# Retention heads in pairs, one in each 64-row half of TensorE's array, with one row tile moved from ACT to DVE

## The chip, the cores and the metric

The kernel runs on one core of a Trainium2 chip. The metric is the device time of one execution in microseconds (us). Before the change three runs took 2376.03, 2383.02 and 2388.97 us; the median is 2383.02. TensorE (PE) multiplies matrices into PSUM, VectorE (DVE) and ScalarE (ACT) read PSUM, GpSimd (POOL) works on SBUF, and SyncE (SP) issues most DMAs.

## The reference, cut to what matters

The program is a stack of eight layers on a sequence of 2048 tokens with 128 channels: softmax attention, a spline network, retention, the spline network again, linear attention, attention with a mixture of experts, a scan over time, and attention with experts again. The change touches the retention layer alone. For each of its 16 heads it needs, with q and k of 8 channels a head and a causal decay,

```
scores[t, s] = q[t] . k[s] * decay[t - s] / scale[t]        for s <= t, else 0
den[t]       = clip(sum over s of |scores[t, s]|, 1, 50000)
out[t]       = (sum over s of scores[t, s] * v[s]) / den[t]
```

followed by a norm over each head's 16 values and a gate. The decay is folded into q and k beforehand. The products with v of earlier token tiles come from a running state in an earlier stage; the stage changed here computes the sums of absolute values (they have no such short form, so every score below the diagonal is made) and the products with v of each token's own 128-token tile.

## The kernel before, in words

`retention_heads_stage` (L1727) takes the heads one after the other. The sequence is cut into 16 row tiles of 128 tokens. q and k of a head are split into high and low parts and so fill 32 rows (`KROWS`) of SBUF; rows 32 to 127 of `qm` and `km` are zero, and each product runs over all 128 rows of the array. There are two buffers, one a head, chosen by `par`.

For one head PE makes three kinds of products:

- "a" units (L1873): one row tile against up to 1024 earlier tokens, into one of two PSUM slots of two banks. ACT sums their absolute values in place (L1920). There are 11: row tiles 5 to 15.
- "d" units, into a ring of three PSUM banks (`DRING`). The first four hold the 16 diagonal tiles, four in a bank (L1883); DVE masks them into `sm` (L1949). The other 14 are what ACT doesn't take, up to 512 columns each (L1887): row tiles 1 to 4, and the part beyond 1024 tokens of row tiles 9 to 15. DVE sums their absolute values (L1955).
- the head's own output (`own_out`, L1852 and L1853): products of the masked scores and of their positive parts with v. They are made a head late, in four pieces, one behind each of d units 8 to 11 of the next head, in 32-column strips of the array. ACT copies the result (L1912), PE turns it with four transposes (`turn_out`, L1861, behind d unit 14), and DVE adds it to `ret` (`take_out`, L1940 and L1941, behind d unit 16).

PE's order is one written list, `order`: the a units are spread evenly among the d units. An a unit waits until ACT has read the unit two before it; a d unit waits until DVE has read the unit three before it. PE executes in this order, so a wait for one of them holds up everything behind it, the pieces of `own_out` too.

SP loads each head's rows with four DMAs (L1789, L1790) of 16 rows of 8 KB; before loading into a buffer it waits until PE is done with the head two before. The first two heads' loads are issued when the stage begins, and PE starts on a head when its four have landed (L1865). POOL makes the positive parts (L1827) and multiplies the gate (L1820).

The attention stages, which the change does not touch, keep two heads at a time in SBUF rows 0 to 63 and 64 to 127 and run products of 64 rows in either half of the array; lines L1175 and L1223 are theirs, and the trace shows their form as 64*128.

Of the kernel before, what the change touches and what calls it, by code (L numbers as in the profile page):

```python
# [18 lines left out]
ALU = mybir.AluOpType  # L19
# [80 lines left out]
def rounded(ap):  # L100

    return ap.bitcast(F32R)
# [1624 lines left out]
def retention_heads_stage(k, w, v, parts_dram, part, diag, ret, gate, x):  # L1727
# [21 lines left out]
    with ExitStack() as ctx:  # L1749
# [17 lines left out]
        PADDED = (slice(KROWS, 2 * KROWS), slice(2 * KROWS, P))  # L1767
# [11 lines left out]
        with nc.Block() as block:  # L1779

            @block.sync
            def _(sp):
                def body(h, par, first=False):
                    if not first:
                        sp.wait_ge(a_full.sem, a_full.at(h * NA - NA))
                        sp.wait_ge(d_full.sem, d_full.at(h * NV - NV))
                    for a in range(PARTS):
                        at = slice(a * PARTS * D, (a + 1) * PARTS * D)
                        sp.dma_start(qm[at, par, :], bcast(q_rows[h, a], 0, PARTS)).then_inc(loaded[par].sem, 16)  # L1789
                        sp.dma_start(km[at, par, :], k_rows[h]).then_inc(loaded[par].sem, 16)  # L1790

                wait_parts(sp, stored)
                body(0, 0, first=True)
                body(1, 1, first=True)
                with sp.Fori(1, H // 2) as n:
                    for par in range(2):
                        body(2 * n + par, par)

            @block.gpsimd
            def _(pool):  # L1800
                for par in range(2):
                    for n, rows in enumerate(PADDED):
                        nc.gpsimd.memset(km[rows, par, :], 0.0).then_inc(k_padded.sem, 1)
                        pool.wait_ge(k_padded.sem, k_padded.at(2 * par + n + 1))
                nc.gpsimd.memset(part[:], 0.0).then_inc(cleared.sem, 1)
                pool.wait_ge(cleared.sem, cleared.at(1))
                nc.gpsimd.memset(twice[:], 0.0).then_inc(cleared.sem, 1)
                pool.wait_ge(cleared.sem, cleared.at(2))
                nc.gpsimd.memset(twice[:, VD:VD + 1], 2.0).then_inc(cleared.sem, 1)
# [6 lines left out]
                def gate_head(h):  # L1816

                    pool.wait_ge(o_used.sem, o_used.at(2 * h + 1))
                    g, r = (t[:, :, bass.ds(h * VD, VD)] for t in (gate, ret))
                    nc.gpsimd.tensor_tensor(g, g, r, ALU.mult).then_inc(gated.sem, 1)  # L1820

                def body(h, par, first=False):
# [3 lines left out]
                    nc.gpsimd.tensor_copy(vh[:, par, :, 0:VD], v[:, :, bass.ds(h * VD, VD)]).then_inc(v_ready.sem, 1)  # L1826
# [3 lines left out]
                body(0, 0, first=True)  # L1830
                body(1, 1, first=True)
                nc.gpsimd.tensor_tensor(x[:], x[:], bcast(w["b_o"][:], 1, NT), ALU.add).then_inc(biased.sem, 1)
                with pool.Fori(1, H // 2) as n:
                    for par in range(2):
                        gate_head(2 * n + par - 2)
                        body(2 * n + par, par)
                gate_head(H - 2)
                gate_head(H - 1)

            @block.tensor  # L1840
            def _(pe):
# [19 lines left out]
                        ins = nc.tensor.transpose(o_ps[:, j * P:(j + 1) * P], ot[:, j * P:(j + 1) * P], w["ident"][:])  # L1861
                    ins.then_inc(o_turned.sem, 1)

                def body(h, turn, par, first=False, second=False):
                    pe.wait_ge(loaded[par].sem, loaded[par].at(turn * NL + NL))  # L1865
                    for kind, n in order:
                        if kind == "a":
                            slot = (par * NA + n) % 2
# [11 lines left out]
                        if n < ND:  # L1880
                            for s in range(QC):
                                i = n * QC + s
                                ins = nc.tensor.matmul(out[:, s * P:(s + 1) * P], rounded(km[:, par, i * P:(i + 1) * P]),  # L1883
                                                       rounded(qm[:, par, i * P:(i + 1) * P]), start=True, stop=True)
                        else:
                            i, at, width = DVEU[n - ND]
# [6 lines left out]

                pe.wait_ge(q_padded.sem, q_padded.at(4))
                pe.wait_ge(k_padded.sem, k_padded.at(4))
                body(0, 0, 0, first=True)
                body(1, 0, 1, second=True)
                with pe.Fori(1, H // 2) as n:
                    for par in range(2):
                        body(2 * n + par, n, par)  # L1900
                for piece in range(NQ):
                    own_out(H - 1, 1, piece)
                turn_out(H - 1)
# [26 lines left out]
            def _(dve):  # L1930
# [5 lines left out]
                def take_out(h):  # L1936
                    dve.wait_ge(o_turned.sem, o_turned.at(h + 1))
                    o = o_ps[:].rearrange("p (t e) -> p t e", e=OW)
                    r = ret[:, :, bass.ds(h * VD, VD)]
                    nc.vector.tensor_tensor(r, o[:, :, 0:VD], r, ALU.add).then_inc(o_used.sem, 1)  # L1940
                    nc.vector.tensor_copy(diag[:, bass.ds(h, 1), :], o[:, :, VD]).then_inc(o_used.sem, 1)  # L1941

                def body(h, par, first=False, first_two=False):
                    for n in range(NV):
                        dve.wait_ge(d_full.sem, d_full.at(h * NV + (n + 1)))
                        if n < ND:
# [3 lines left out]
                                                    d_ps[n % DRING][:].rearrange("p (s t) -> p s t", t=P), bcast(w["keep_kq"][:], 1, QC),  # L1950
                                                    ALU.mult).then_inc(d_used.sem, 1)
                        else:
                            i, at, width = DVEU[n - ND]
                            slot = 1 + (at // BANK) % 2
                            nc.vector.tensor_reduce(part[:, bass.ds(h, 1), i, slot:slot + 1], d_ps[n % DRING][:, 0:width], AX.X, ALU.add,  # L1955
                                                    apply_absolute_value=True).then_inc(d_used.sem, 1)
                        if n == READ_AT and not first:
                            take_out(h - 1)

                body(0, 0, first=True, first_two=True)  # L1960
                body(1, 1, first_two=True)
                with dve.Fori(1, H // 2) as n:
                    for par in range(2):
                        body(2 * n + par, par)
                take_out(H - 1)

        for par in range(2):
            loaded[par].done(NL * H // 2)
        cleared.done(5)
        q_padded.done(4)  # L1970
        k_padded.done(4)
# [682 lines left out]
```

## Time and profile before

| | us | share of the span |
|---|---|---|
| median of the three runs | 2383.02 | |
| the profiled execution | 2386.77 | |
| its span, first to last instruction | 2385.0 | 100% |
| PE busy | 1936.0 | 81% |
| DVE busy | 1677.1 | 70% |
| ACT busy | 1374.0 | 58% |
| POOL busy | 455.2 | 19% |
| PE's own products of the stage begin and end | 657.1 to 878.6 | 9% |

The shares are means over stages that differ. Matmuls are pipelined and their ends are modelled, so PE can read as busy for nearly the whole of a stretch; the start times of its instructions tell more. The granted clock is 1.00 at 2.4 GHz and 0.50 at 1.2 GHz.

### The profile page before, as it was taken

To read this page: it belongs to the slowest core of one execution; us is meant where nothing else is said; L and a number is where in the kernel's file an instruction comes from. 1 tells how busy PE (TensorE), PEld (TensorE's weight loads), DVE (VectorE), ACT (ScalarE), POOL (GpSimd) and SP (SyncE) were. 2 spreads that over 40 slices of the span, in tenths; PEclk is the share of its full clock that TensorE was granted. 3 is DMA by queue.
4 is the path that set the end of the run, shared out by engine and by line. 5 is a ranking of instruction groups with operands and counts; after the bars stand their busy time and mean duration, and the time that the engine had idled before them with its cause. 6 is when DMAs were issued, how large, how long until landed. Compare 5 with 4: busy or idle time off the path is not lost. (4 is left out here: it accounts for less than half of the span.)

```text
span 2385.0 us, 38939 instructions
## 1 busy us (share of the span) xinstructions
PE 1936.0 (81%) x12970; PEld 1046.3 (44%) x12970; DVE 1677.1 (70%) x4201; ACT 1374.0 (58%) x2027; POOL 455.2 (19%) x816
## 2 busy tenths in 40 slices
PE   5899899975699974687899899957557999999839
PEld 3433333333477753464333333337334333333338
DVE  6688798747466777567798898632696897888423
ACT  4257667865378865435367677832543466677712
POOL 4010120110245430220101110133000010211233
PEclk8599999996899986897699999978865799999959
DMA  7342020001201000006032020014024402200034
GB/s 218 81 72 37 3 38 2 2 33 32 79 38 40 38 18 1 1 1 174 17 59 38 3 38 2 2 47 176 25 59 118 72 13 26 38 2 2 2 106 159
DMA packets 47527, 113.89 MB, mean 48 GB/s; under 512 B 11952, under 2 KB 21426, under 8 KB 43144
## 3 DMA queue, kind: packets, MB, share of 16 engines
q1 hardware_dynamic: 40308, 96.84, 17.2%
q0 software_dynamic: 5088, 11.24, 1.5%
q10 hardware_dynamic: 1964, 3.70, 0.4%
q8 instruction: 90, 1.47, 0.3%
q14 instruction: 77, 0.63, 0.1%
HBM read 62.39 MB, written 32.64 MB: 40 GB/s over the span
## 5 line engine op out<-in xcount | busy, mean ns | idle before, releaser
L1124 ACT ACTIVATE probs<-score 128x1024 f32<-128x1024 f32 x960 | 822.8, 897 | 429.1 <-PE score L1223 423.1
L1294 DVE TENSOR_REDUCE max_part<-stat 128x1 f32<-128x512 f32 x1152 | 724.7, 682 | 94.0 <-PE stat L1175 86.2
L1237 PE MATMUL pv<-probs,v_ones 128*9 128x512 f32 (+3 forms) x3840 | 458.4, 551 | 0.6 <-ACT out_turned L1117 0.6
L1291 DVE CUSTOM_DVE_ANT_0 masked_scores<-stat,mask_row 128x128 f32<-128x128 f32 (+3 forms) x768 | 346.8, 487 | 145.3 <-PE stat L1175 142.2
L1175 PE MATMUL stat<-first_group_k,first_group_q 64*128 64x512 f32 (+2 forms) x960 | 364.2, 496 | 41.5 <-PEq L708 16.1
L1175 PE MATMUL stat<-group_k,group_q 64*128 64x512 f32 (+2 forms) x960 | 337.4, 407 | 16.2 <-DVE max_part L1294 7.7
L1175 PEld LDWEIGHTS stat<-first_group_k,first_group_q 64*128 64x128 f32 x960 | 176.7, 215 | 288.3 <-DVE max_part L1294 174.6
L1175 PEld LDWEIGHTS stat<-group_k,group_q 64*128 64x128 f32 x960 | 157.8, 185 | 279.2 <-DVE max_part L1294 162.1
L1223 PE MATMUL score<-first_group_q,first_group_k 64*128 64x512 f32 x960 | 251.3, 423 | 32.0 <-ACT probs L1124 19.6
L1223 PE MATMUL score<-group_q,group_k 64*128 64x512 f32 x960 | 229.8, 418 | 40.4 <-ACT probs L1124 31.3
L1920 ACT ACTIVATE abs_act_ps<-abs_act_ps 128x1024 f32<-128x1024 f32 (+3 forms) x176 | 167.5, 952 | 46.8 <-PE abs_act_ps L1873 43.2
L1082 POOL TENSOR_SCALAR_AFFINE_SELECT probs<-probs 128x256 f32<-128x256 f32 x384 | 149.6, 406 | 233.9 <-ACT probs L1124 232.5
L1223 PEld LDWEIGHTS score<-first_group_q,first_group_k 64*128 64x128 f32 x960 | 132.1, 199 | 53.4 <-ACT probs L1124 29.8
L1955 DVE TENSOR_REDUCE abs_part<-abs_dve_ps 128x512 f32 (+5 forms) x224 | 109.0, 515 | 61.2 <-PE abs_dve_ps L1887 61.1
L1223 PEld LDWEIGHTS score<-group_q,group_k 64*128 64x128 f32 x960 | 112.7, 185 | 89.4 <-ACT probs L1124 84.5
L1873 PE MATMUL abs_act_ps<-head_k,head_q 128*128 128x512 f32 x352 | 118.4, 423 | 1.3 <-ACT abs_act_ps L1920 0.2
L1091 POOL CAST row_max_parts<-row_max 128x16 fp32r<-128x16 f32 x48 | 9.4, 197 | 560.4 <-DVE row_max L1268 560.4
L1237 PEld LDWEIGHTS pv<-probs,v_ones 128*9 128x9 f32 x3840 | 57.4, 88 | 121.1 <-issue 89.5
L2430 DVE TENSOR_TENSOR hidden<-value_ps,gate 128x512 f32<-128x512 f32 x38 | 26.3, 691 | 118.0 <-PE value_ps L2334 116.5
L1099 POOL TENSOR_TENSOR qkv<-out_rows,inv_denominator 128x128 f32<-128x128 f32 x48 | 19.5, 406 | 373.3 <-DVE inv_denominator L1275 373.3
L1827 POOL TENSOR_SCALAR own_positive<-own_scores 128x2048 f32<-128x2048 f32 x16 | 85.8, 5360 | 0.0
L1887 PE MATMUL abs_dve_ps<-head_k,head_q 128*128 128x512 f32 (+2 forms) x224 | 72.1, 347 | 0.0
(369 smaller groups left out, 2488.7 us busy)
## 6 DMA issues: line engine op xcount, KB each, us to landing
tile_wv<-expert_wv SPq DMA_DIRECT2D x38, 512.0 KB, 3.2
q_parts<-early_parts_t SPq DMA_DIRECT2D x21, 512.0 KB, 3.8
k_parts<-early_parts_t SPq DMA_DIRECT2D x12, 512.0 KB, 4.7
group_k<-k_parts SPq DMA_DIRECT2D x24, 256.0 KB, 11.9
group_q<-q_parts SPq DMA_DIRECT2D x24, 256.0 KB, 18.2
head_q<-q_parts SPq DMA_DIRECT2D x32, 128.0 KB
head_k<-k_parts SPq DMA_DIRECT2D x32, 128.0 KB
first_group_q<-pad_rows SPq DMA_DIRECT2D x6, 512.0 KB, 5.6
```

The source lines that it names most:

```text
L1082: nc.gpsimd.affine_select(tile, tile, [[0, 2], [1, P]], ALU.is_ge, 0.0, base=0, channel_multiplier=-1).then_inc(cut.sem, 1)
L1124: nc.scalar.activation(probs[:, n % PSLOTS, :, 0:width], sc[m % 2][:, :, 0:width], ACT.Exp, scale=scale).then_inc(slot_read.sem, 1)
L1175: nc.tensor.matmul(ring[n % RBANKS][:, 0:width], rounded(uq[b][rows, h // 2, at:at + P]), rounded(uk[b][rows, h // 2, c * BANK:c * BANK + ...
L1223: last = nc.tensor.matmul(sc[m % 2][:, i, 0:BANK - f], rounded(uk[b][rows, hp, kt * P:(kt + 1) * P]), rounded(uq[b][rows, hp, j * BANK + f ...
L1237: last = nc.tensor.matmul(acc[32 * h:32 * h + D + 1, f:BANK], v9[:, kt, g * HG + h, :], probs[:, (2 * t + h // 2) % PSLOTS, h % 2, 0:BANK ...
L1291: nc.vector.tensor_tensor_reduce(masked[:, at % 2, 0:width], ring[n % RBANKS][:, 0:width], w["mask_row"][:, BANK - width:BANK], 1.0, NEG, ...
L1294: nc.vector.reduce_max(into, ring[n % RBANKS][:], AX.X).then_inc(stat_used.sem, 1)
L1827: nc.gpsimd.tensor_scalar(sa[:, par, :], sm[:, par, :], 0.0, None, ALU.max).then_inc(abs_ready.sem, 1)
L1873: ins = nc.tensor.matmul(a_ps[slot][:, b:min(b + BANK, width)], rounded(qm[:, par, i * P:(i + 1) * P]), rounded(km[:, par, at + b:at + min ...
L1887: ins = nc.tensor.matmul(out[:, 0:width], rounded(qm[:, par, i * P:(i + 1) * P]), rounded(km[:, par, at:at + width]), start=True, stop=True)
L1920: nc.scalar.activation(ps, ps, ACT.Abs, accum_out=part[:, bass.ds(h, 1), i, 0:1]).then_inc(a_used.sem, 1)
L1955: nc.vector.tensor_reduce(part[:, bass.ds(h, 1), i, slot:slot + 1], d_ps[n % DRING][:, 0:width], AX.X, ALU.add, apply_absolute_value=True) ...
```

## The change

Heads are loaded in pairs: head 2p into rows 0 to 63 of a buffer, head 2p+1 into rows 64 to 127, with 32 real and 32 zero rows each. A buffer now holds a pair, a pair takes eight DMAs, and PE waits for all eight before it starts on the pair. Each product runs over 64 rows at a stated position of the array. Per pair there are two passes. In the first, a units take the head in the lower half and d units (with the own output that follows from them) the head in the upper half; in the second they are exchanged. ACT's loop is as it was, since ACT now takes the heads in order while DVE, POOL and the own output take them as 1, 0, 3, 2 and so on. Row tile 6, until now an a unit of 768 columns, becomes three d units of 256 columns; a head has 10 a units and 21 d units. The list `order`, the places of the own-output pieces (behind d units 8 to 11), of the transposes (14) and of `take_out` (16) keep their formulas. The zero rows cleared are now 32 to 63 and 96 to 127.

```diff
-    ACTU = [(i, 0, min(i * P, LONG)) for i in range(5, NT)]
+    SPLIT = 6
+    ACTU = [(i, 0, min(i * P, LONG)) for i in range(5, NT) if i != SPLIT]
     DVEU = []
     for i in range(1, NT):
         at = 0 if i < 5 else LONG
+        if i == SPLIT:
+            DVEU += [(i, n * 2 * P, 2 * P, n) for n in range(SPLIT // 2)]
         while at < i * P:
-            DVEU.append((i, at, min(BANK, i * P - at)))
+            DVEU.append((i, at, min(BANK, i * P - at), 1 + (at // BANK) % 2))
             at += BANK
...
-        NL = 2 * PARTS * 16
+        NL = 2 * 2 * PARTS * 16
+        TURNS = H // 4
...
-                def body(h, par, first=False):
+                def load_pair(p, buf, first=False):
                     if not first:
-                        sp.wait_ge(a_full.sem, a_full.at(h * NA - NA))
-                        sp.wait_ge(d_full.sem, d_full.at(h * NV - NV))
-                    for a in range(PARTS):
-                        at = slice(a * PARTS * D, (a + 1) * PARTS * D)
-                        sp.dma_start(qm[at, par, :], bcast(q_rows[h, a], 0, PARTS)).then_inc(loaded[par].sem, 16)
-                        sp.dma_start(km[at, par, :], k_rows[h]).then_inc(loaded[par].sem, 16)
+                        sp.wait_ge(a_full.sem, a_full.at(p * 2 * NA - 2 * NA))
+                        sp.wait_ge(d_full.sem, d_full.at(p * 2 * NV - 2 * NV))
+                    for half in range(2):
+                        for a in range(PARTS):
+                            at = slice(half * HROWS + a * PARTS * D, half * HROWS + (a + 1) * PARTS * D)
+                            sp.dma_start(qm[at, buf, :], bcast(q_rows[p * 2 + half, a], 0, PARTS)).then_inc(loaded[buf].sem, 16)
+                            sp.dma_start(km[at, buf, :], k_rows[p * 2 + half]).then_inc(loaded[buf].sem, 16)
...
-                def body(h, turn, par, first=False, second=False):
-                    pe.wait_ge(loaded[par].sem, loaded[par].at(turn * NL + NL))
+                def body(h, turn, seat, first=False, second=False):
+                    buf, par = seat // 2, seat % 2
+                    here, other = (slice(HROWS * half, HROWS * half + HROWS) for half in (par, 1 - par))
+                    if par == 0:
+                        pe.wait_ge(loaded[buf].sem, loaded[buf].at(turn * NL + NL))
...
-                                ins = nc.tensor.matmul(a_ps[slot][:, b:min(b + BANK, width)], rounded(qm[:, par, i * P:(i + 1) * P]),
-                                                       rounded(km[:, par, at + b:at + min(b + BANK, width)]), start=True, stop=True)
+                                ins = nc.tensor.matmul(a_ps[slot][:, b:min(b + BANK, width)], rounded(qm[here, buf, i * P:(i + 1) * P]),
+                                                       rounded(km[here, buf, at + b:at + min(b + BANK, width)]), start=True, stop=True,
+                                                       tile_position=(here.start, 0))
...
-                            ins = nc.tensor.matmul(out[:, 0:width], rounded(qm[:, par, i * P:(i + 1) * P]), rounded(km[:, par, at:at + width]), start=True, stop=True)
+                            ins = nc.tensor.matmul(out[:, 0:width], rounded(qm[other, buf, i * P:(i + 1) * P]), rounded(km[other, buf, at:at + width]),
+                                                   start=True, stop=True, tile_position=(other.start, 0))
```

## Rows read from the trace of the kernel before

**Rows 1.** Busy time by engine, 13 heads; columns: stretch, engines, PEclk, DMA share, GB/s
```profile
672.20:847.00 174.80, 173.50 (x1558) 126.47 (x1557) 123.90 (x259) 150.37 (x300) 87.84 (x39) 1.00 0.10 39
```
**Rows 2.** Waits, 686 to 862 us; columns: us in total, times, longest
```profile
DVE abs_part L1955 <- PE abs_dve_ps L1887: 50.6, 91, 0.9
...
ACT abs_act_ps L1920 <- PE abs_act_ps L1873: 22.5, 28, 1.2
```
**Rows 3.** Timeline of SP, first load of the third and last head; columns: start, us
```profile
672.20 0.66 SPq L1789 DMA_DIRECT2D head_q<-q_parts  x1
...
847.09 0.65 SPq L1789 DMA_DIRECT2D head_q<-q_parts  x1
```
**Rows 4.** Timeline of PE within one head, around two own-output pieces
```profile
730.78 0.22 PE L1887 MATMUL abs_dve_ps<-head_k,head_q 128*128 128x128 f32 x1
730.93 0.45 PE L1852 MATMUL own_out_ps<-own_scores,ret_v_head 128*32 128x128 f32 x8
...
731.53 0.73 PE L1873 MATMUL abs_act_ps<-head_k,head_q 128*128 128x512 f32 x2
732.10 0.28 PE L1887 MATMUL abs_dve_ps<-head_k,head_q 128*128 128x256 f32 x1
732.31 0.45 PE L1852 MATMUL own_out_ps<-own_scores,ret_v_head 128*32 128x128 f32 x8
```
**Rows 5.** Groups by line and shape, 686 to 862 us; busy, mean ns, idle before
```profile
L1920 ACT ACTIVATE abs_act_ps<-abs_act_ps 128x1024 f32<-128x1024 f32 x105 | 106.1, 1011 | 19.2 <-PE abs_act_ps L1873 16.0
...
L1955 DVE TENSOR_REDUCE abs_part<-abs_dve_ps 128x512 f32 x65 | 44.8, 689 | 27.0 <-PE abs_dve_ps L1887 27.0
...
L1949 DVE TENSOR_TENSOR own_scores<-abs_dve_ps,keep_kq 128x512 f32<-128x512 f32 x52 | 32.7, 683 | 1.5 <-PE abs_dve_ps L1883 1.3
...
L1955 DVE TENSOR_REDUCE abs_part<-abs_dve_ps 128x384 f32 x39 | 21.6, 553 | 12.5 <-PE abs_dve_ps L1887 12.5
L1955 DVE TENSOR_REDUCE abs_part<-abs_dve_ps 128x256 f32 x39 | 16.4, 421 | 11.1 <-PE abs_dve_ps L1887 11.1
...
L1955 DVE TENSOR_REDUCE abs_part<-abs_dve_ps 128x128 f32 x39 | 11.0, 283 | 0.0
...
L1920 ACT ACTIVATE abs_act_ps<-abs_act_ps 128x768 f32<-128x768 f32 x13 | 10.3, 795 | 5.1 <-PE abs_act_ps L1873 5.1
```
**Rows 6.** Timeline of DVE in the same head
```profile
732.52 0.42 DVE L1955 TENSOR_REDUCE abs_part<-abs_dve_ps 128x256 f32 x1 [0.84 <-PE abs_dve_ps L1887]
...
736.00 0.89 DVE L1955 TENSOR_REDUCE abs_part<-abs_dve_ps 128x512 f32 x2 [0.33 <-PE abs_dve_ps L1887]
...
739.33 0.41 DVE L1940 TENSOR_TENSOR ret_out<-own_out_ps,ret_out 128x256 f32 x1
...
739.75 0.55 DVE L1955 TENSOR_REDUCE abs_part<-abs_dve_ps 128x384 f32 x1
```
**Rows 7.** Timeline of PE in an attention stage, products of 64 rows
```profile
200.00 0.49 PE L1175 MATMUL stat<-group_k,group_q 64*128 64x512 f32 x1
200.01 0.72 PE L1223 MATMUL score<-first_group_q,first_group_k 64*128 64x512 f32 x2
200.35 0.39 PE L1175 MATMUL stat<-group_k,group_q 64*128 64x512 f32 x1
200.57 0.40 PE L1223 MATMUL score<-first_group_q,first_group_k 64*128 64x512 f32 x2
```
**Rows 8.** PE's first product of the stage in its timeline
```profile
657.14 1.09 PE L1883 MATMUL abs_dve_ps<-head_q,head_k 128*128 128x128 f32 x4 [13.19 <-DMA head_k<-k_parts]
```
**Rows 9.** Busy time in two stretches of the stage's start, columns as rows 1
```profile
646.30:656.50 10.20, 0.00 (x0) 0.00 (x0) 5.87 (x4) 0.00 (x0) 7.60 (x9) 0.50 0.12 50
656.50:666.50 10.00, 9.36 (x33) 8.52 (x34) 4.92 (x9) 4.48 (x9) 3.56 (x2) 0.50 0.13 53
```
**Rows 10.** Busy time in stretches of an attention stage, columns as rows 1
```profile
1900.00:1920.00 20.00, 18.09 (x116) 7.00 (x108) 18.63 (x42) 10.06 (x13) 3.48 (x10) 1.00 0.30 37
2007.90:2014.70 6.80, 6.45 (x30) 2.29 (x30) 2.69 (x12) 3.37 (x5) 0.00 (x0) 0.50 0.01 2
```

More of the change, by code:

```diff
@@ L1782, in _ @@
             def _(sp):
-                def body(h, par, first=False):
+                def load_pair(p, buf, first=False):
                     if not first:
-                        sp.wait_ge(a_full.sem, a_full.at(h * NA - NA))
-                        sp.wait_ge(d_full.sem, d_full.at(h * NV - NV))
-                    for a in range(PARTS):
-                        at = slice(a * PARTS * D, (a + 1) * PARTS * D)
-                        sp.dma_start(qm[at, par, :], bcast(q_rows[h, a], 0, PARTS)).then_inc(loaded[par].sem, 16)
-                        sp.dma_start(km[at, par, :], k_rows[h]).then_inc(loaded[par].sem, 16)
-                wait_parts(sp, stored)
[L1793 to L1797, printed above, removed]
+                        sp.wait_ge(a_full.sem, a_full.at(p * 2 * NA - 2 * NA))
[5 more added lines that the diff above has]
+                            sp.dma_start(km[at, buf, :], k_rows[p * 2 + half]).then_inc(loaded[buf].sem, 16)
+                wait_parts(sp, stored)
+                load_pair(0, 0, first=True)
+                load_pair(1, 1, first=True)
+                with sp.Fori(1, TURNS) as n:
+                    for buf in range(2):
+                        load_pair(2 * n + buf, buf)
             @block.gpsimd
@@ L1814, in _, with gate_head, body @@
                 pool.wait_ge(cleared.sem, cleared.at(5))
-                def gate_head(h):
+                def gate_head(h, head):
                     pool.wait_ge(o_used.sem, o_used.at(2 * h + 1))
-                    g, r = (t[:, :, bass.ds(h * VD, VD)] for t in (gate, ret))
+                    g, r = (t[:, :, bass.ds(head * VD, VD)] for t in (gate, ret))
                     nc.gpsimd.tensor_tensor(g, g, r, ALU.mult).then_inc(gated.sem, 1)
-                def body(h, par, first=False):
+                def body(h, head, par, first=False):
                     if not first:
@@ L1825, in body @@
                     pool.wait_ge(d_used.sem, d_used.at(h * NV + ND))
-                    nc.gpsimd.tensor_copy(vh[:, par, :, 0:VD], v[:, :, bass.ds(h * VD, VD)]).then_inc(v_ready.sem, 1)
+                    nc.gpsimd.tensor_copy(vh[:, par, :, 0:VD], v[:, :, bass.ds(head * VD, VD)]).then_inc(v_ready.sem, 1)
                     nc.gpsimd.tensor_scalar(sa[:, par, :], sm[:, par, :], 0.0, None, ALU.max).then_inc(abs_ready.sem, 1)
                     pool.wait_ge(abs_ready.sem, abs_ready.at(h + 1))
-                body(0, 0, first=True)
-                body(1, 1, first=True)
+                body(0, 1, 0, first=True)
+                body(1, 0, 1, first=True)
                 nc.gpsimd.tensor_tensor(x[:], x[:], bcast(w["b_o"][:], 1, NT), ALU.add).then_inc(biased.sem, 1)
@@ L1882, in body @@
                                 i = n * QC + s
-                                ins = nc.tensor.matmul(out[:, s * P:(s + 1) * P], rounded(km[:, par, i * P:(i + 1) * P]),
-                                                       rounded(qm[:, par, i * P:(i + 1) * P]), start=True, stop=True)
-                        else:
-                            i, at, width = DVEU[n - ND]
-                            ins = nc.tensor.matmul(out[:, 0:width], rounded(qm[:, par, i * P:(i + 1) * P]), rounded(km[:, par, at:at + width]), start=True, stop=True)
+                                ins = nc.tensor.matmul(out[:, s * P:(s + 1) * P], rounded(km[other, buf, i * P:(i + 1) * P]),
+                                                       rounded(qm[other, buf, i * P:(i + 1) * P]), start=True, stop=True, tile_position=(other.start, 0))
+                        else:
+                            i, at, width, _ = DVEU[n - ND]
+                            ins = nc.tensor.matmul(out[:, 0:width], rounded(qm[other, buf, i * P:(i + 1) * P]), rounded(km[other, buf, at:at + width]),
+                                                   start=True, stop=True, tile_position=(other.start, 0))
                         ins.then_inc(d_full.sem, 1)
@@ L1895, in _ @@
                 pe.wait_ge(k_padded.sem, k_padded.at(4))
[L1896 to L1900, printed above, removed]
+                for seat in range(4):
+                    body(seat, 0, seat, first=seat == 0, second=seat == 1)
+                with pe.Fori(1, TURNS) as n:
+                    for seat in range(4):
+                        body(4 * n + seat, n, seat)
                 for piece in range(NQ):
@@ L1934, in _, with take_out, body @@
                 dve.wait_ge(cleared.sem, cleared.at(1))
-                def take_out(h):
+                def take_out(h, head):
                     dve.wait_ge(o_turned.sem, o_turned.at(h + 1))
                     o = o_ps[:].rearrange("p (t e) -> p t e", e=OW)
-                    r = ret[:, :, bass.ds(h * VD, VD)]
+                    r = ret[:, :, bass.ds(head * VD, VD)]
                     nc.vector.tensor_tensor(r, o[:, :, 0:VD], r, ALU.add).then_inc(o_used.sem, 1)
-                    nc.vector.tensor_copy(diag[:, bass.ds(h, 1), :], o[:, :, VD]).then_inc(o_used.sem, 1)
-                def body(h, par, first=False, first_two=False):
+                    nc.vector.tensor_copy(diag[:, bass.ds(head, 1), :], o[:, :, VD]).then_inc(o_used.sem, 1)
+                def body(h, head, before, par, first=False, first_two=False):
                     for n in range(NV):
@@ L1952, in body @@
                         else:
-                            i, at, width = DVEU[n - ND]
-                            slot = 1 + (at // BANK) % 2
-                            nc.vector.tensor_reduce(part[:, bass.ds(h, 1), i, slot:slot + 1], d_ps[n % DRING][:, 0:width], AX.X, ALU.add,
+                            i, at, width, slot = DVEU[n - ND]
+                            nc.vector.tensor_reduce(part[:, bass.ds(head, 1), i, slot:slot + 1], d_ps[n % DRING][:, 0:width], AX.X, ALU.add,
                                                     apply_absolute_value=True).then_inc(d_used.sem, 1)
                         if n == READ_AT and not first:
-                            take_out(h - 1)
-                body(0, 0, first=True, first_two=True)
-                body(1, 1, first_two=True)
+                            take_out(h - 1, before)
+                body(0, 1, None, 0, first=True, first_two=True)
+                body(1, 0, 1, 1, first_two=True)
                 with dve.Fori(1, H // 2) as n:
                     for par in range(2):
-                        body(2 * n + par, par)
-                take_out(H - 1)
+                        body(2 * n + par, 2 * n + 1 - par, 2 * n - 2 + 3 * par, par)
+                take_out(H - 1, H - 2)
         for par in range(2):
-            loaded[par].done(NL * H // 2)
+            loaded[par].done(NL * TURNS)
         cleared.done(5)
```

12 lines of the change are left out of this document (6 added, 6 removed).

## The prediction, made before the changed kernel ran

> **What bounds the stage now.** I read the busy time of thirteen whole heads first, then the waits, then PE's timeline in one head. The thirteen heads take 174.9 us from SP's first load for the third head to its first for the last, 13.45 us each [rows 3]. In them PE is busy 173.5 of 174.8 us, ACT 150.4, DVE 123.9, at clock 1.00 [rows 1]. Every large wait of the stage points the same way: DVE waited 50.6 us for PE's d units, ACT 22.5 us for its a units [rows 2]. So PE sets 13.45 us a head, DVE has 3.9 us a head to spare (174.8 less 123.9, over 13) and ACT 1.9. PE's start times show why: its products stand in single file, and where an own-output piece comes, PE gives 0.60 us to it (730.93 to 731.53), during which neither reader is fed [rows 4].
>
> **Products of 64 rows.** The attention stages show what the change relies on. A stat product and a score product in different halves start at 200.00 and 200.01, the next pair at 200.35, the next at 200.57 [rows 7]: two 512-column products run side by side, a pair every 0.22 us where weights are loaded ahead, and 0.33 us after a wait, 0.11 more, because the weights are loaded first. I take this over. In the new order two products of an a unit stand in one half, then d products in the other, so the second of each group runs beside the first of the next. Single file is then no bound except around the own-output pieces. What is late next has to be walked through.
>
> **One head after the change.** ACT's floor: 150.4/13 = 11.57 us less tile 6, 0.80 [rows 1, 5], 10.8 us. DVE's: 123.9/13 = 9.53 plus three times 256 columns. A sum of 256 columns lasts 0.42 us, but neighbours overlap by 0.08: two of 512 and 128 columns take 0.89, where 0.689 and 0.283 make 0.97 [rows 5, 6]. So DVE's steps are 0.61, 0.47, 0.34 and 0.20 us for 512, 384, 256 and 128 columns, 0.60 for a masked diagonal bank, and 0.41 for take_out (739.33 to 739.75) [rows 5, 6]. DVE's floor is 9.53 + 3 x 0.34 = 10.6 us. The two floors are nearly equal, but a head can't reach them, since PE alternates between a stretch where it feeds both and a stretch with the four own-output pieces where it feeds them little.
>
> - The own-output stretch, from the first piece to the first product behind the fourth. Four pieces, 0.60 each: 2.40. Between the first two stands one d unit of 256 columns: it hands over to the next piece after 0.21 (732.10 to 732.31) plus 0.11 for its weights, 0.32. Then an a unit of 0.57 (731.53 to 732.10) with a d unit beside its second product, plus 0.10 to hand over, 0.67. Then a d unit of 128 columns, 0.15 (730.78 to 730.93) plus 0.11, 0.26 [rows 4]. Sum 3.65 us. DVE has four short units here, 1.2 us of work, and then idles.
> - Behind it DVE gets d unit 12 beside the second product of a unit 5: 0.34 until that starts, 0.28 for it, 0.15 to DVE (732.10 + 0.28 to 732.52) [rows 4, 6], 0.77 us. From there it must sum d units 12 to 20 and 0 to 5 of the next head before unit 5's bank is free for unit 8, which PE issues ahead of the next first piece: three of 256, two of 384, four of 512, two of 128 columns, take_out and four diagonal banks: 1.02 + 0.94 + 2.44 + 0.40 + 0.41 + 2.40 = 7.61 us. The transposes behind unit 14 hold up unit 15; my estimate from their place between two waits is 0.2 us. Unit 8 then needs 0.05 to be released, 0.11 for weights and 0.21 to the piece, 0.37. Sum 0.77 + 7.81 + 0.37 = 8.95 us.
> - ACT has in the same stretch a copy of 512 columns, 0.6 (an estimate, over half of the 1.01 for 1024 columns), and seven units, at most 1.01 each [rows 5], 7.65 us, so it is behind DVE there, and DVE is the one that decides.
>
> Together 12.6 us a head, 0.85 less than before; for fifteen heads -12.8 us. I take these terms to be good to 0.4 us a head, 6 us. Moving tile 6 costs DVE 1.03 us and frees ACT of 0.80; its three units fall on DVE's idle own-output stretch, but push units that stood there into the stretch that DVE decides, so I count no gain for the move.
>
> The Trainium skill, TensorEngine Tiling (Array Packing), Key Properties, says that a change of tiling mode drains TensorE. The transposes use the whole array, so they would add two more such changes a head; in rows a piece and the product behind it cost 0.60, of which the drain is a part [rows 4]. At 0.2 us each on the path it would be 0.4 x 16 = 6 us. I leave it out of the sum, since PE waits for DVE there.
>
> **The first pair's load.** Before, PE starts at 657.14, released by the fourth DMA of head 0 after 13.19 us without work [rows 8]. The DMA engines are busy 0.12 and 0.13 of 16 from 646.3 to 666.5, about two engines at 50 GB/s, with no gap [rows 9]: the eight first DMAs go through one after the other, four in the first 10.2 us, four in the next 10. PE used the first four at once and the next a head later. Now it waits for all eight: it starts at 667.1, 9.9 us later, with nothing to hide it. Bounds: 0 if DMAs to rows 64 and up went beside the others, 10 as here. I take 9.9, because rows 0 to 15 and 16 to 31 already show no such thing. Later pairs: eight DMAs take 20 us, two heads 25, so they stay hidden.
>
> **The first head.** It has no own output before it. It took 657.14 to 672.20, 15.1 us [rows 3, 8], the first 9.4 at clock 0.50 [rows 9] with PE busy all of it. With pairs of products side by side PE is less of a bound; DVE's and ACT's floors are 10.6 and 10.8, the four diagonal banks go at the slow clock as before. I estimate 12.3, with 10.8 and 15.1 as bounds: -2.8 us.
>
> SP's issues are as many as before, and POOL's 87.8/13 = 6.8 us a head [rows 1] stays hidden in 12.6.
>
> **Sum**, against the profiled execution of 2386.8: -12.8 - 2.8 + 9.9 = -5.7, 2381.1. The median of the runs is 3.8 lower: 2377. About 0.5%, 12 us, is what a measurement of this kernel can tell from no change, so this counts as no change.
>
> **Rivals.**
> - The heads run at the floors. If rings of three and two banks bridge the own-output stretch better than I walk it, a head takes 10.8 us: -2.65 x 15 = -39.8, with the other terms -32.7, 2350; halfway, 11.7 us, 2364. For it: the two floors now match. Against: three banks hold 1 us of DVE's work, the stretch 3.65. The Trainium skill, TensorEngine Tiling (Array Packing), PSUM Bottleneck, says that tiling speeds up TensorE and not the emptying of PSUM; by that rule alone the floors are what is left, and the time is this rival's.
> - No overlap. If the halves don't run side by side in this order (two products in one half, then the other), PE stays the bound at 13.45 plus one more product, 13.55: +1.5 + 9.9 = +11.4, 2394. Against: the pairs at 200.35 and 200.57 [rows 7].
> - The clock falls, and the kernel gets slower. The stage ran at 1.00 with PE in whole-array products and busy throughout [rows 1]. With products of 64 rows an attention stage held 1.00 with PE busy 18.1 of 20 us, but 108 us later stood at 0.50 for 6.8 us [rows 10]. After the change PE waits for DVE in much of a head. At 0.50 the own-output stretch alone goes from 3.65 towards 7, so a head costs some 4 us more (estimate). It decides from two cold heads on, which eat the gain of 5.7; with five of sixteen cold it is +14, 2397; with all, +58.
>
> **Chances.** My forecast 0.48 (2368 to 2389), the floors 0.20, no overlap 0.12, the clock 0.15, others 0.05. Faster by over 0.5%: all of the floors and a fifth of the forecast, 0.30. Slower: two thirds of the clock, half of no overlap, 0.04 of the rest, 0.20. Within: 0.50. Range 2358 to 2397: it leaves the lower half of the floors and the worse half of the clock outside.
>
> **What would show it.** PE's first product of the stage at 667 instead of 657, with a wait for a DMA of about 23 us. Starts of L1873 and L1887 within 0.02 us of each other. DVE's waits for PE, 50.6 us before, down to about 2.5 us a head and all around the own-output pieces; PE's waits now on DVE. SP's loads for two pairs 25.2 us apart. It is wrong if the loads are under 23.5 us or over 26.5 apart, if PE starts well before 667, or if the clock in the stage is not 1.00.

## The result: slower by 3.5%

| | before | after |
|---|---|---|
| median of the runs, us | 2382.81 (2376.03 to 2388.97) | 2464.89 (2453.57 to 2479.27) |
| span of the profiled execution | 2385.0 | 2461.5 |
| mean granted clock of the span | 0.877 | 0.833 |
| PE busy / DVE busy / ACT busy | 1936.0 / 1677.1 / 1374.0 | 2000.0 / 1695.3 / 1366.8 |
| PE's first to last product of the stage | 657.1 to 878.6 (221.5) | 671.6 to 961.5 (289.8) |

The ratio of the times is 1.0348, with the interval 1.0296 to 1.0400. The forecast of 2377 and its range, up to 2397, are both missed, on the slow side.

The span grew by 76.5 us. The stage itself became 68.3 us longer. It also began later: between the last product of the stage before and its own first one lie 23.6 us, where 13.2 lay, which is 10.4. The unchanged stages account for the remaining -2.2 (the one before the heads ended 4.1 us later, those behind took 6.3 less).

Busy time of the changed kernel, columns as in [rows 1]: two short stretches, 40 us further on in two pieces, and the whole stage.

```profile
718.00:724.80 6.80, 6.51 (x40) 4.33 (x40) 6.20 (x15) 5.75 (x12) 0.74 (x1) 1.00 0.13 53
...
752.10:759.00 6.90, 6.37 (x42) 4.44 (x40) 6.74 (x15) 6.50 (x13) 0.72 (x1) 0.99 0.13 52
...
760.00:780.00 20.00, 20.00 (x135) 13.90 (x136) 12.01 (x27) 12.32 (x24) 7.97 (x5) 0.50 0.04 13
800.00:820.00 20.00, 20.00 (x139) 13.93 (x138) 11.28 (x24) 11.13 (x21) 7.73 (x4) 0.50 0.04 17
...
671.62:961.46 289.84, 287.48 (x1936) 199.26 (x1936) 171.34 (x366) 177.69 (x336) 107.06 (x48) 0.55 0.07 26
```

[Rows 1] had 1.00 over thirteen heads. Here the stage has 0.55: 258.0 of its 289.8 us stand at 0.50, that is at 1.2 GHz, and in those PE is busy 20.00 of 20.00 us while DVE and ACT have some 8 us to spare. In the short stretches at 2.4 GHz DVE is busier (6.20 of 6.80 and 6.74 of 6.90) and PE has pauses (6.51 and 6.37).

Waits of the changed kernel, 700 to 920 us, columns as in [rows 2]:

```profile
DVE abs_part L1965 <- PE abs_dve_ps L1897: 83.0, 72, 1.9
ACT abs_act_ps L1931 <- PE abs_act_ps L1882: 66.3, 81, 2.6
...
PEld abs_dve_ps L1897 <- DVE abs_part L1965: 17.8, 50, 0.5
```

DVE's and ACT's waits for PE have grown, from 50.6 and 22.5 us in thirteen heads [rows 2] to 83.0 and 66.3 in the twelve that 220 us now hold. PE was to be relieved, and is the bound more than before.

PE's timeline in the changed kernel: the start of the stage, as [rows 8], two products side by side, as [rows 7], and the own-output stretch with the first product behind it, as [rows 4].

```profile
671.62 1.30 PE L1893 MATMUL abs_dve_ps<-head_q,head_k 64*128 64x128 f32 x5 [23.57 <-DMA head_k<-k_parts]
...
826.34 0.79 PE L1897 MATMUL abs_dve_ps<-head_k,head_q 64*128 64x512 f32 x1
826.34 0.79 PE L1882 MATMUL abs_act_ps<-head_k,head_q 64*128 64x512 f32 x1
...
835.78 0.67 PE L1857 MATMUL own_out_ps<-own_scores,ret_v_head 128*32 128x128 f32 x8
836.20 0.68 PE L1858 MATMUL own_out_ps<-own_positive,twice_sum 128*32 128x128 f32 x8
836.81 0.58 PE L1897 MATMUL abs_dve_ps<-head_k,head_q 64*128 64x256 f32 x1
837.32 0.67 PE L1857 MATMUL own_out_ps<-own_scores,ret_v_head 128*32 128x128 f32 x8
...
841.96 0.79 PE L1882 MATMUL abs_act_ps<-head_k,head_q 64*128 64x512 f32 x1
```

The halves do run side by side (both products start at 826.34), but a product of 512 columns lasts 0.79 us here and 0.49 in [rows 7]. A piece comes 1.54 us after the one before it (835.78 to 837.32), and the whole stretch lasts 841.96 - 835.78 = 6.18 us.

SP's first loads for the third and the eighth pair, as [rows 3]:

```profile
704.00 0.67 SPq L1794 DMA_DIRECT2D head_q<-q_parts  x1
...
885.34 0.62 SPq L1794 DMA_DIRECT2D head_q<-q_parts  x1
```

Five pairs in 181.3 us are 36.3 us a pair and 18.1 a head, where 13.45 stood.

### The profile page after: what moved, and what is told of

Same layout as the page of the kernel before. It is cut to its first block and busy times, and to the rows that moved or that the text cites. A ratio compares the mean times of both kernels' runs of the same rounds, so it can differ in the third digit from the quotient of the medians.

```text
span 2461.5 us, 38949 instructions
## 1 busy us (share of the span) xinstructions
PE 2000.0 (81%) x12986; PEld 1078.6 (44%) x12986; DVE 1695.3 (69%) x4249; ACT 1366.8 (56%) x1995; POOL 456.2 (19%) x816
## 3 DMA queue, kind: packets, MB, share of 16 engines
q8 instruction: 94, 1.54, 0.3%
## 5 line engine op out<-in xcount | busy, mean ns | idle before, releaser
L1175 PE MATMUL stat<-first_group_k,first_group_q 64*128 64x512 f32 (+2 forms) x960 | 360.3, 485 | 43.9 <-PEq L708 16.1
L1175 PE MATMUL stat<-group_k,group_q 64*128 64x512 f32 (+2 forms) x960 | 337.0, 406 | 16.2 <-DVE max_part L1294 7.6
L1175 PEld LDWEIGHTS stat<-first_group_k,first_group_q 64*128 64x128 f32 x960 | 173.5, 211 | 291.3 <-DVE max_part L1294 179.2
L1175 PEld LDWEIGHTS stat<-group_k,group_q 64*128 64x128 f32 x960 | 157.2, 184 | 277.7 <-DVE max_part L1294 161.1
L1223 PE MATMUL score<-first_group_q,first_group_k 64*128 64x512 f32 x960 | 246.8, 417 | 32.0 <-ACT probs L1124 19.5
L1223 PE MATMUL score<-group_q,group_k 64*128 64x512 f32 x960 | 231.6, 422 | 40.0 <-ACT probs L1124 30.6
L1931 ACT ACTIVATE abs_act_ps<-abs_act_ps 128x1024 f32<-128x1024 f32 (+2 forms) x160 | 154.7, 967 | 111.8 <-PE abs_act_ps L1882 109.3
L1965 DVE TENSOR_REDUCE abs_part<-abs_dve_ps 128x256 f32 (+6 forms) x272 | 124.9, 498 | 106.5 <-PE abs_dve_ps L1897 105.0
L1882 PE MATMUL abs_act_ps<-head_k,head_q 64*128 64x512 f32 x320 | 165.0, 632 | 0.3 <-ACT abs_act_ps L1931 0.2
L1223 PEld LDWEIGHTS score<-group_q,group_k 64*128 64x128 f32 x960 | 113.4, 187 | 92.8 <-ACT probs L1124 85.7
L1223 PEld LDWEIGHTS score<-first_group_q,first_group_k 64*128 64x128 f32 x960 | 129.7, 196 | 53.2 <-ACT probs L1124 29.7
L1897 PE MATMUL abs_dve_ps<-head_k,head_q 64*128 64x256 f32 (+3 forms) x272 | 124.9, 547 | 1.2 <-DVE own_scores L1960 1.1
L1882 PEld LDWEIGHTS abs_act_ps<-head_k,head_q 64*128 64x128 f32 x320 | 78.3, 291 | 21.3 <-issue 11.5
## 6 DMA issues: line engine op xcount, KB each, us to landing
group_k<-k_parts SPq DMA_DIRECT2D x24, 256.0 KB, 11.9
group_q<-q_parts SPq DMA_DIRECT2D x24, 256.0 KB, 18.1
```

The source lines that it names most:

```text
L1175: nc.tensor.matmul(ring[n % RBANKS][:, 0:width], rounded(uq[b][rows, h // 2, at:at + P]), rounded(uk[b][rows, h // 2, c * BANK:c * BANK + ...
L1223: last = nc.tensor.matmul(sc[m % 2][:, i, 0:BANK - f], rounded(uk[b][rows, hp, kt * P:(kt + 1) * P]), rounded(uq[b][rows, hp, j * BANK + f ...
L1897: ins = nc.tensor.matmul(out[:, 0:width], rounded(qm[other, buf, i * P:(i + 1) * P]), rounded(km[other, buf, at:at + width]), start=True, ...
L1931: nc.scalar.activation(ps, ps, ACT.Abs, accum_out=part[:, bass.ds(h, 1), i, 0:1]).then_inc(a_used.sem, 1)
L1965: nc.vector.tensor_reduce(part[:, bass.ds(head, 1), i, slot:slot + 1], d_ps[n % DRING][:, 0:width], AX.X, ALU.add, apply_absolute_value=Tr ...
```

## The experiments

Two theories for the low clock. By the first, it follows how many of the array's rows the products run over: 64 instead of 128. By the second, it follows PE's pauses: PE now waits for DVE in each head. Both were named in the third rival, which did not separate them. Each experiment's time is shown beside the kernel before on the same chip. Where no ratio is given the kernel ran once; 19 runs of the kernel before reach from 2371.39 to 2399.28 us, so a few us in a single run show nothing by themselves.

**64 rows alone, and pauses alone.** The first kernel has nothing of pairs: heads in single file as before, but each score product over rows 0 to 63 (the edit of one of three lines, cut):

```diff
...
-rounded(qm[:, par, i * P:(i + 1) * P]), rounded(km[:, par, at:at + width]), start=True, stop=True)
+rounded(qm[0:HROWS, par, i * P:(i + 1) * P]), rounded(km[0:HROWS, par, at:at + width]), start=True, stop=True, tile_position=(0, 0))
```

> The kernel before with every score product cut to 64 of its 128 rows (rows 0 to 63, one half of the array); the rows left out held zeros. Same order, same counts, one head at a time, no overlap. Theory A (the granted clock follows how much of the array's height the products use): the clock falls to 0.50 in most of the stage and, as PE sets the pace in single file, a head goes from 13.4 us to 20 or more: 2383 + 100 or more. Theory B (the clock falls because PE waits for DVE and ACT once its products overlap; rows don't matter): PE is as busy as before, clock 1.00, 2383 within 0.5%.

The second keeps the 128 rows and makes DVE sum each of its 14 units of a head twice, so that PE must wait (the line that sets up `spare` is left out):

```diff
...
+nc.vector.tensor_reduce(spare[:, n:n + 1], d_ps[n % DRING][:, 0:width], AX.X, ALU.add, apply_absolute_value=True)
```

> The kernel before with products of all 128 rows, but DVE takes each of its 14 sums of a head twice (the second into a spare column), 6.1 us more, so that DVE sets the pace and PE waits for it in much of a head. Theory A: the clock stays 1.00 and the stage is longer by what DVE needs, 16 to 17 us a head, 2383 + 40 to 60. Theory B: the clock falls to 0.50 in much of the stage, as in the changed kernel, and a head takes 18 us or more: over 2460.

Measured: 2532.59 and 2412.7 us, beside 2387.71. Busy time of the products of 64 rows, and below it of the doubled sums:

```profile
657.00:1020.00 363.00, 363.00 (x1849) 269.86 (x1849) 163.45 (x314) 192.06 (x364) 106.29 (x47) 0.50 0.06 22
```
```profile
660.00:760.00 100.00, 92.84 (x700) 66.84 (x699) 93.94 (x213) 73.76 (x146) 45.88 (x20) 0.91 0.08 33
760.00:860.00 100.00, 93.72 (x763) 67.70 (x760) 93.28 (x211) 72.35 (x143) 41.10 (x19) 0.91 0.08 34
```

With products of 64 rows the clock stays at 0.50, where it stood when the stage began, for 367.4 of its 369.4 us, with PE busy without a pause. With 128 rows and a PE that pauses 7 us in 100, the clock is at 0.50 for 39.7 of 258.9 us: 9.0 at the start, as in the kernel before (9.3), and 30.7 in seven short falls. So the rows alone are enough to keep the clock down, and pauses alone bring a small part of it. The first time is as theory A has it. The second is below both ranges, though a head took 16.0 us (twelve heads' loads, 191.5 us), as A says. The Trainium skill, TensorE: Matmul & The Clock Gate, Part 1: The HAM clock gate, says that the gate goes by how busy the PE has been; by that the first kernel would have run at 2.4 GHz, and the measurement decides: busy 363.00 of 363.00 us (as modelled), at 1.2.

**The parts of the change.** Pairs without the move of tile 6 (`SPLIT = 0`), and the move without pairs (the lists ACTU and DVEU of the change on the kernel before):

> The change without moving row tile 6: pairs in halves, 11 a units and 18 d units as before. If the pairs cost the clock (A and B alike), the stage stays at 0.50 for the most part and the time is within 15 us of the changed kernel's 2465. If tile 6, which makes DVE the last one in the stretch behind the own output, is what makes PE wait enough to lose the clock, the time is near 2375 to 2395 at 1.00.

> Row tile 6 moved from ACT to DVE alone, with products of all 128 rows and one head at a time as before. PE sets the pace, one product more a head: 2383 + 2 within 0.5%, clock 1.00, under all theories.

Measured: 2448.0 and 2383.62, beside 2387.71. Busy time, of the pairs alone over the stage, then of the move alone over the same 174.80 us as [rows 1]:

```profile
673.50:940.60 267.10, 261.59 (x1920) 170.84 (x1920) 154.59 (x318) 188.43 (x368) 107.13 (x48) 0.62 0.07 28
```
```profile
672.20:847.00 174.80, 173.94 (x1566) 128.70 (x1564) 134.81 (x298) 140.24 (x273) 88.47 (x40) 1.00 0.10 39
```

The pairs bring the loss (0.62; their time is 17 us below the changed kernel's, where within 15 was expected). In single file, moving tile 6 costs nothing that one run can tell: DVE takes 10.9 us more, ACT 10.1 less, PE stays the bound. In pairs the move makes the low-clock time 258.0 instead of 203.4 us and the stage 22.7 us longer; these runs don't say by what.

**Whole-array products added back.** If rows are the cause, products over all 128 rows beside the pairs must bring the clock back, though they are extra work. The kernels are the changed one with products that nobody reads, at five places in each head, two at each (ten a head) or four (twenty).

```diff
+        FILL_AT, FILLS = (18, 20, 1, 3, 5), 2
...
+                        if n == FILL_AT[0] and not first:
+                            pe.wait_ge(o_used.sem, o_used.at(2 * h))
+                        if n in FILL_AT:
+                            for _ in range(FILLS):
+                                nc.tensor.matmul(o_ps[:], rounded(qm[:, buf, 0:P]), rounded(km[:, buf, 0:BANK]), start=True, stop=True)
```

> The changed kernel with ten products a head more that nobody reads: 128 rows by 512 columns, two ahead of each of d units 18, 20, 1, 3 and 5, into the own output's bank while that is free. They are pure extra work for PE: 10 x 0.21 us at 2.4 GHz and five more pairs of changes of form, some 4 us a head. Theory A (rows at work hold the clock): the clock is 1.00 in more of the stage than in the changed kernel, and if in most of it, a head takes about 14 us in place of 18 and the time falls to 2395 to 2420, though PE has more to do. If the half-height products have nothing to do with the clock: the extra work is done at 0.50, 6 us a head more, 2465 + 60 to 100.

> The same with four ahead of each, twenty a head, 6.4 us of PE's time a head at 2.4 GHz. Theory A: the clock is 1.00 in nearly all of the stage; PE sets the pace at about 16 us a head, 2425 to 2445, still below the changed kernel's 2465. Otherwise: over 2560.

Measured: 2431.14 and 2459.5, beside 2386.53, both above the ranges of theory A, though the clock did what it says. Busy time with ten and with twenty:

```profile
720.00:820.00 100.00, 99.37 (x900) 61.85 (x899) 71.30 (x153) 72.30 (x140) 44.56 (x20) 1.00 0.09 37
```
```profile
700.00:800.00 100.00, 99.34 (x830) 63.70 (x831) 62.28 (x135) 63.97 (x122) 42.87 (x18) 1.00 0.08 31
```

The kernel with 160 products more took 34 us less than the changed one's median (and 22 less than the fastest of its four runs), since its clock is at 1.00 from 696 us to the end of the stage. The time with twenty can't be told from the changed kernel's, but its clock is up as well. With the two runs before, that shows the cause: in this stage it is products over half the rows that keep the clock down. Whether the rows as such count or the work that they make up in a time, the runs don't tell apart.

The two also give an estimate of what a pair costs at 2.4 GHz. SP's first loads for the third and the eighth pair, with ten and with twenty:

```profile
705.91 0.67 SPq L1795 DMA_DIRECT2D head_q<-q_parts  x1
...
855.05 0.62 SPq L1795 DMA_DIRECT2D head_q<-q_parts  x1
```
```profile
712.19 0.67 SPq L1795 DMA_DIRECT2D head_q<-q_parts  x1
...
884.26 0.62 SPq L1795 DMA_DIRECT2D head_q<-q_parts  x1
```

Five pairs in 149.1 and 172.1 us are 14.9 and 17.2 us a head, so ten products more cost 2.3 us, 0.23 each; by the stages (251.7 and 284.9 us, of which 29.8 and 19.1 at 0.50) it is 0.207. Less ten products, a head would take 12.6 to 12.8 us at 1.00. That the first ten cost as much as the next ten is not shown, nor did any run hold 1.00 in pairs without them; as far as the estimate goes, the forecast's 12.6 was the right size for that clock. PE's timeline with ten shows its own-output stretch, too:

```profile
785.39 0.45 PE L1858 MATMUL own_out_ps<-own_scores,ret_v_head 128*32 128x128 f32 x8
...
788.99 0.49 PE L1883 MATMUL abs_act_ps<-head_k,head_q 64*128 64x512 f32 x1
```

3.60 us, where the forecast walked 3.65.

**Fewer changes of mode**, that is between products of 64 rows and products of the whole array. Ten added products a head in two groups of five instead of five groups of two (the first), the same with the four own-output pieces put together behind d unit 8 (the second), and that without the move of tile 6 (the third, its groups ahead of d units 17 and 3):

```diff
-        FILL_AT, FILLS = (18, 20, 1, 3, 5), 2
+        FILL_AT, FILLS = (18, 3), 5
...
-                        if PV_AT <= n < PV_AT + NQ and not first:
-                            own_out(h - 1, 1 - par, n - PV_AT, first=second)
+                        if n == PV_AT and not first:
+                            for piece in range(NQ):
+                                own_out(h - 1, 1 - par, piece, first=second)
```

> The changed kernel with the ten unread whole-array products a head in two groups of five, ahead of d units 18 and 3, in place of five groups of two: the same work, three changes of form fewer each way. Theory A (height at work holds the clock): clock 1.00 in most of the stage; PE then has some 3 us a head more than in the changed kernel, about what it was forecast to idle in the stretch that DVE decides, so a head takes 12.6 to 13.5 us, the forecast's walk with a small addition, and the time is 2385 to 2405. If groups this far apart don't hold the clock: 0.50 in part of the stage, 2420 to 2500.

> The same, and the four own-output pieces together behind d unit 8. At clock 1.00 the own-output stretch shrinks from 3.65 to about 2.3 us, PE's work is about 11.5 us a head, and DVE's and ACT's floors of 10.6 and 10.8 are near: 11.5 to 12.2 us a head, 16 x -1.2 to -1.9 against the kernel before, +10 for the first pair's load and a longer slow start: 2365 to 2380, faster than the kernel before. If the clock isn't held: over 2420.

> The same without the move of row tile 6 (11 a units, 18 d units; the groups ahead of d units 17 and 3). ACT's floor is 11.6 us a head, DVE's 9.5. If ACT decides at 1.00, a head takes 12.0 to 12.6 and the time is 4 to 10 us above the run with tile 6 moved; if PE decides, the same within 3 us.

Measured: 2423.21, 2429.62 (ratio 1.0206, 1.0166 to 1.0247) and 2480.25 (1.0394, 1.0342 to 1.0447), beside 2382.45. All three expectations missed: the first time lies in the range given for a lost clock, but the clock was held. Busy time of the three:

```profile
700.00:860.00 160.00, 153.47 (x1364) 98.26 (x1364) 109.85 (x243) 115.06 (x223) 70.23 (x33) 1.00 0.09 34
```
```profile
720.00:860.00 140.00, 130.28 (x1194) 86.45 (x1193) 97.83 (x215) 99.57 (x197) 59.39 (x28) 1.00 0.09 36
```
```profile
700.00:900.00 200.00, 188.20 (x1311) 125.74 (x1311) 97.29 (x203) 118.07 (x234) 69.03 (x31) 0.69 0.07 27
```

The first two held 1.00, but a head took 15.2 and 15.1 us (loads of five pairs, 152.0 and 151.1), no less than with five places of two, although PE now pauses 4 and 7 us in 100. I had taken the added products to fall into pauses; a head became no shorter for it. The two bear on the second theory, too: PE is busy 96 and 93 us in 100 here, and in the changed kernel's short stretches at 1.00 it was 96 and 92 (6.51 of 6.80, 6.37 of 6.90). There the clock fell each time, here it held, so pauses of this size alone don't explain the fall. The third did not hold the clock (0.69) with as many added products. Why, these runs don't say.

**Blocks in single file.** The kernel before with the four pieces together (the edit above), and with tile 6 moved as well:

> The kernel before with whole-array products; only the four own-output pieces stand together behind d unit 8 in place of one behind each of units 8 to 11. Three changes of form less each way: some 0.3 us each on PE, which sets the pace: 13.4 to 12.5 us a head, 2383 - 10 to - 15, clock 1.00. If the readers starve behind the longer block (1.9 us; ACT's two slots hold 2.0 us, DVE's three banks 1.0 to 1.8), the gain is under 5 us.

> The same with row tile 6 moved from ACT to DVE as well, whole-array products. PE has one product a head more, ACT 0.8 us less to do. If PE alone sets the pace, the time is that of the run before within 3 us; if ACT (11.6 us a head of work, stalls besides) has become the bound there, this one is 5 to 10 us faster, 2363 to 2370.

Measured: 2381.54, ratio 0.9988 (0.9959 to 1.0017), and 2378.52, ratio 0.9967 (0.9944 to 0.9991), beside 2386.53. Busy time of the two over the same 174.80 us as [rows 1]:

```profile
672.20:847.00 174.80, 169.65 (x1571) 130.40 (x1570) 123.09 (x264) 149.91 (x303) 89.14 (x42) 1.00 0.10 40
```
```profile
672.20:847.00 174.80, 172.87 (x1594) 132.30 (x1594) 139.33 (x304) 139.43 (x278) 88.53 (x40) 1.00 0.10 40
```

The first can't be told from no change: PE got time to spare (169.65 busy instead of 173.50 [rows 1]), while ACT is as busy as before, 149.91. With tile 6 moved DVE and ACT are even, 139.33 and 139.43, and the stage takes 216.1 us instead of 221.5. The second is 0.3% faster than the kernel before. That it is faster than the first (3.0 us between the medians) is not shown. The gain of 10 to 15 us expected of the first did not come, and the second lies between its two cases.

**Three quarters of the rows.** The kernel before, products over rows 0 to 95, no halves (again one of three lines):

```diff
...
-rounded(qm[:, par, i * P:(i + 1) * P]), rounded(km[:, par, at:at + width]), start=True, stop=True)
+rounded(qm[0:96, par, i * P:(i + 1) * P]), rounded(km[0:96, par, at:at + width]), start=True, stop=True)
```

> The kernel before with every product of the retention heads over rows 0 to 95 instead of 0 to 127 (rows 32 to 95 are zero as before), in the mode of the whole array and in single file; no pairs, tile 6 with ACT. Theory A1 (the clock follows the share of the array's rows that the products run over): three quarters is between the kernel before (1.00) and the products of 64 rows (0.50 for 367 of 369 us), so the clock is at 0.50 for a part of the stage, 60 to 250 us, and the time is 2405 to 2480 us. Theory A2 (it is the division of the array into halves that counts, each half by itself): the products here use the undivided array, the clock stays at 1.00 but for some 9 us, and the time is that of before, 2378 to 2392 us.

Measured: 2386.77, beside 2374.13. Busy time:

```profile
667.00:677.00 10.00, 10.00 (x33) 8.55 (x33) 6.04 (x11) 7.14 (x14) 1.49 (x1) 0.50 0.02 4
...
687.00:697.00 10.00, 10.00 (x51) 7.36 (x43) 4.28 (x9) 5.63 (x10) 2.97 (x2) 0.53 0.00 0
697.00:707.00 10.00, 9.99 (x104) 7.30 (x104) 6.93 (x14) 8.05 (x18) 6.19 (x3) 1.00 0.11 43
...
780.00:880.00 100.00, 99.47 (x908) 72.59 (x908) 70.64 (x149) 86.01 (x171) 50.09 (x23) 1.00 0.09 37
```

Neither expectation holds as put: of the first, time and low-clock time are both too high; of the second the time holds, but not the 9 us. The clock stayed at 0.50 for the first 39.4 us of the stage, where the kernel before had 9.3 and the other four kernels with 128 rows 8.6 to 9.0, so the rows count without any division into halves; once at 1.00, it stayed there to the end. The effect lies between those of 64 and 128 rows, nearer to 128. Products of 64 rows without a stated position were not tried.

## Why the prediction was wrong

- **The step that failed** is the clock at which a head was walked. Every term of "One head after the change" comes from rows at 1.00, and the walk puts PE's products at that pace. The stage ran at 0.55. That the clock falls stood there as the third rival, at 0.15, with a wrong reason: "PE waits for DVE in much of a head". The single-file kernel of 64 rows, which had no pause, shows the rows to be enough, and two of the kernels with added products held 1.00 with pauses as large as the changed kernel's.
- **The rival's price was too small.** It made a low-clock head 4 us dearer than 12.6, mostly from the own-output stretch going "towards 7"; with all heads low, +58. A head took 18.1 us, 5.5 dearer. The stretch is 6.18 us; the other 18.1 - 6.18 = 11.9 us stand where the walk had 8.95 at DVE's pace. At 1.2 GHz PE becomes the bound there too (20.00 of 20.00 busy), and this the rival left out.
- **The sign** was in the same trace, but hardly in [rows 10]. The 6.80 us there at 0.50 come behind 7.90 us in which PE had pauses (the first line below), and the other row of the group has products of 64 rows at 1.00. The start of another attention stage speaks more clearly (the second line), and its further course points the other way (the third):

```profile
2000.00:2007.90 7.90, 6.61 (x51) 2.98 (x48) 7.23 (x25) 5.22 (x8) 1.59 (x5) 1.00 0.01 3
...
1155.00:1178.00 23.00, 22.95 (x88) 10.51 (x84) 17.15 (x42) 9.79 (x11) 0.00 (x0) 0.50 0.00 0
...
1180.00:1560.00 380.00, 348.72 (x2402) 139.12 (x2402) 309.07 (x789) 270.22 (x340) 55.45 (x157) 1.00 0.17 24
```

With products of 64 rows (L1175, L1223) among its work PE hardly paused for 23 us, and the clock stayed at 0.50, where the heads' stage of the same kernel, with 128 rows, was at 1.00 after 9.3 us. Once up, that attention stage held 1.00 for 380 us. So products of 64 rows don't always bring 1.2 GHz, and what sets the attention stages apart from the changed one is not shown.

- **The overlap** came as taken from [rows 7]; the second rival fell.
- **The head at 1.00.** 12.6 to 12.8 us, an estimate from the two kernels with added products, against 12.6: within the 0.4 given. The own-output stretch was 3.60 against 3.65. In the changed kernel's stretches at 1.00 DVE was the busier reader (6.74 of 6.90), as said; that it alone sets the pace there is not shown. No kernel came near the floors' 10.8 a head.
- **The first pair's load**: +10.4 us against +9.9, and a wait of 23.57 where about 23 was said.
- **The first head**: -2.8 could not be seen; the first pair took 32.4 us (671.6 to 704.0), all of it at 0.50.
- **Tile 6** is neutral alone, as the forecast counted it; in pairs it went with 54.6 us more at 0.50.
- **The sum at 1.00** was nearly no change. Carried down to no added products the stage with ten would take 251.7 - 33.2 = 218.5 us, or 214.9 at 0.23 us a product (an estimate), 3.0 to 6.6 less than before, against 10.4 us of later start. By this estimate pairs would not have paid at 1.00 either; no run shows it.

## What to carry to other kernels

Before products are cut to half the array's height, ask for the granted clock of every stretch of the same kernel that already runs such products with PE busy, the starts of stages above all, and price the whole stage at 1.2 GHz, every stretch walked anew, not only the one that PE sets now. Rows of zeros that look wasted can be what keeps the clock up. Where two readers wait in turn for a PE that works in single file, evening out their loads and putting side jobs together gained 0.3% (0.1% to 0.6%) without touching the array.

## What the runs showed of the hardware

- Rows of zeros count: in the kernel before, rows 32 to 127 of both operands are zero and the clock holds 1.00 [rows 1]; with products that leave out 64 of these 96 rows it stays at 0.50 for 367.4 of 369.4 us. In an attention stage of the kernel before, where products of 64 rows in the two halves and others take turns, 1.00 was held for 380 us.
- Work added can take time away: with 160 whole-array products that nobody reads the changed kernel took 34 us less (2431.14, one run, against a median of 2464.89).
- With 96 rows the clock rose 39.4 us after the stage's first product, with 128 after 9.3; once up, both held it.
- The four kernels that start the stage with products of 64 rows and later hold 1.00 (those with added products) came up late as well: 19.1 to 29.8 us of 0.50 in the stage, where products of 128 rows had 8.6 to 9.3.
